# Key maxima and square sums placed among the value tiles, scatters placed beside late gathers, logit groups placed anew

## The reference, cut to what matters

```python
# attention over random features; dn = 64 ** -0.25
dash = einsum('bhnd,md->bhnm', data * dn, proj)
diag = 0.5 * dn ** 2 * sum(data * data, axis=-1)
stab = max(dash, -1) if is_query else max(dash, (-2, -1))   # keys: one maximum per head
feature = ratio * (exp(dash - diag - stab) + EPS)

# graph attention, edges src -> dst
msg = xl[src] + xr[dst]
e = einsum('ehd,hd->eh', where(msg > 0, msg, 0.2 * msg), att)
alpha = softmax of e over the edges of each dst
out = segment_sum(alpha * xl[src], dst) @ W_up
```

## Time and profile before

| what | us |
|---|---|
| median of three runs | 1893.53 |
| lowest and highest | 1887.46, 1898.96 |
| the profiled execution, whole | 1897.03 |
| its span on the core | 1895.2 |
| TensorE busy in it | 1792.2 (95%) |
| VectorE, ScalarE, GpSimd busy | 744.7, 390.4, 644.6 |

### The profile page before, as it was taken

How to read it: one execution, slowest core, us unless ns; L and a number is a source line. 1 busy time by engine, 2 the same in 40 slices (tenths; PEclk the granted TensorE clock), 3 DMA queues, 4 the chain that set the end, 5 groups by cost and what they waited for, 6 DMA issues and landing times. The chain is left out here.

```text
span 1895.2 us, 22157 instructions
## 1 busy us (share of the span) xinstructions
PE 1792.2 (95%) x8594; PEld 1140.2 (60%) x8594; DVE 744.7 (39%) x1523; ACT 390.4 (21%) x715; POOL 644.6 (34%) x538
## 2 busy tenths in 40 slices
PE   7999999998999999999999999999999999999953
PEld 5466445544554777546677765677654676676731
DVE  5967101332524322454455557340530223222226
ACT  0000000001401011001576745211000312222222
POOL 0566881030000076777887620000300222222210
PEclk9999999999999999999899999999999999999986
DMA  9645115073530144333222145150321799999952
GB/s 344 182 113 144 2 2 155 22 223 66 214 129 5 32 123 133 92 96 86 54 54 53 37 101 154 45 223 24 102 94 45 253 415 407 401 411 410 404 161 88
DMA packets 104070, 289.09 MB, mean 153 GB/s; under 512 B 61942, under 2 KB 65240, under 8 KB 91837
## 3 DMA queue, kind: packets, MB, share of 16 engines
q1 hardware_dynamic: 28634, 224.83, 32.1%
q0 software_dynamic: 68160, 51.85, 12.3%
q10 hardware_dynamic: 7198, 11.36, 1.9%
HBM read 257.19 MB, written 30.32 MB: 152 GB/s over the span
## 5 line engine op out<-in xcount | busy, mean ns | idle before, releaser
L325 PE MATMUL bank<-wring,turned_a 128*125 128x512 f32 x480 | 207.6, 593 | 1.6 <-DVE turned_a L640 0.7
L523 POOL DMA_INDIRECT table_d<-wring x85 | 174.5, 2053 | 97.8 <-issue 63.3
L886 POOL DMA_INDIRECT wring<-xl_d,wring x85 | 109.1, 1284 | 256.4 <-DMA xr_d<-flat_b 230.5
L325 PEld LDWEIGHTS bank<-wring,turned_a 128*125 128x125 f32 x480 | 89.6, 188 | 115.3 <-issue 114.2
L2154 PEld LDWEIGHTS bank<-picked_t,wring 128*128 128x128 f32 x1280 | 145.3, 194 | 7.6 <-issue 7.3
L2154 PE MATMUL bank<-picked_t,wring 128*128 128x128 f32 x1280 | 147.2, 278 | 0.1
L341 PE MATMUL bank<-flat_d,wring 128*128 128x312 f32 (+1 forms) x512 | 135.0, 426 | 0.0
L899 POOL DMA_INDIRECT score_d<-wring x85 | 110.8, 1303 | 69.7 <-DMA score_d<-wring 47.0
L886 POOL DMA_INDIRECT wring<-xr_d,wring x85 | 111.9, 1317 | 25.9 <-issue 25.9
L341 PEld LDWEIGHTS bank<-flat_d,wring 128*128 128x128 f32 x512 | 96.7, 189 | 37.9
L2169 PE MATMUL bank<-wring,unit_t 128*128 128x512 f32 x160 | 74.0, 605 | 0.0
(11 more groups left out here) (433 smaller groups left out, 2764.8 us busy)
## 6 DMA issues: line engine op xcount, KB each, us to landing
wring<-in_experts SPq DMA_DIRECT2D x60, 2048.0 KB, 13.1
wring<-in_L_Ws SPq DMA_DIRECT2D x6, 2048.0 KB, 19.3
table_d<-eq_buf SPq DMA_DIRECT2D x2, 3072.0 KB, 30.1
score_d<-no_edge SPq DMA_DIRECT2D x2, 3072.0 KB, 33.3
wring<-table_d POOLq DMA_DIRECT2D x10, 610.4 KB, 7.3
wring<-score_d SPq DMA_DIRECT2D x5, 1093.8 KB
wring<-pid_d ACTq DMA_DIRECT2D x17, 312.5 KB
wring<-in_edge_w ACTq DMA_DIRECT2D x17, 312.5 KB
```

The lines of the kernel that those rows point to most:

```text
L325: ins = pe.matmul(bank[0:R, :], act_t[:, k, tok(t)], w[:, k * HALF:(k + 1) * HALF], start=(k == 0), stop=(k == chunks - 1))
L523: pool.indirect_dma_start(out=tables_d[b % 2], out_offset=bass.IndirectOffsetOnAxis(ap=edge_at[:, b:b + 1], axis=0), in_=edge_sums[:, b, : ...
L886: pool.indirect_dma_start(out=to[:, g % 2, j, :], out_offset=None, in_=table, in_offset=bass.IndirectOffsetOnAxis(ap=index[:, b:b + 1], ax ...
```

## The change

It has four parts.

- **Key maxima.** Ten key products follow each of the first eight value tiles, none the last two. The loop over value tiles is written out on both engines, and TensorE waits for all keys ahead of the first tile.
- **Square sums.** Keys come first. For each pair of chunks the squares are the moving operand, in two pieces of 313 and 312 columns, and 64 columns of `pair_sel` the weights; the two chunks of the pair go to the lower and the upper 64 rows of a bank. One pair follows the key products of each of the first eight tiles (32 products in all). VectorE copies the sums (`keep_sums`) after tiles 3 and 7, TensorE turns them (`turn_sums`) after tiles 5 and 8, and VectorE sorts them into `neg_k` and `neg_q`. The chain of the maximum stands around tiles 8 and 9.
- **Gathers and scatters.** GpSimd gathers blocks 10 to 39 without scatters. From block 40 on there is a scatter ahead of each gather, as long as the scatters stay ten blocks behind; the rest follow at the end.
- **Logit groups.** Groups 0 to 7 stand ahead of the value tiles, group 8 behind tile 4, group 9 behind tile 8, groups 10 to 16 in attention from u = 2, 12, 22, 33, 45, 58 and 70.

```diff
@@ -846,7 +846,7 @@
-SCATTER_LAG = 13
+SCATTER_FROM, SCATTER_LAG = 40, 10
@@ -870,19 +870,23 @@
+sums = context_flat[:, 0:N]
...
-def gather_block(pool, b):
+def gather_block(pool, b, beside=None):
...
+        if beside:
+            beside()
@@ -937,8 +941,8 @@
-SEL = 100
+SEL = 64
@@ -963,18 +967,21 @@
-KMAX_U = HEADS * T // (2 * T)
+KMAX_U, KMAX_TILES = 2 * T, K
...
-QK_GROUPS = 5
-V_GROUP_AT = {1: 5, 3: 6, 6: 7, 8: 8}
+QK_GROUPS = 8
+V_GROUP_AT = {4: 8, 8: 9}
...
-LATE_STEP_AT = {2 + 10 * g + 2 * n for g in range(GROUPS_E - LATE_GROUP) for n in range(4)}
+LATE_STARTS = (2, 12, 22, 33, 45, 58, 70)
+LATE_STEP_AT = {first + 2 * n for first in LATE_STARTS for n in range(4)}
+SUMS_BANK = {0: 4, 1: 6}
@@ -1121,7 +1128,6 @@
-            pe.wait_ge(s_emptied, keys_made)
@@ -1129,27 +1135,60 @@
-        pe_gemm_rows(pe, x1_t, beside=key_products)
-        pe.wait_ge(v1_set, 5)
-        for side in range(2):
+        def square_sums(pair):
+            pe.wait_ge(squared.sem, 2 * pair + 2)
+            side, at_sel = pair // 4, 6 - 2 * (pair % 4)
+            for n, (at, cols) in enumerate(TOKEN_PIECES):
+                for g in range(2):
+                    ins = pe.matmul(banks[SUMS_BANK[side] + n][g * SEL:(g + 1) * SEL, 0:cols],
+                                    pair_sel[:, at_sel:at_sel + SEL], sq[:, g, at:at + cols],
+                                    start=(pair % 4 == 0), stop=(pair % 4 == 3))
+            ins.then_inc(squares_used, 1)
+        def turn_sums(side):
+            pe.wait_ge(sums_kept, 2 * side + 2)
...
-            for k in range(K):
-                pe.wait_ge(squared.sem, side * K + k + 1)
-                at = HEADS - 2 - 2 * k
-                for t in range(T):
-                    ins = pe.matmul(bank[0:R, t * SEL:(t + 1) * SEL], sq[:, k % 2, tok(t)],
-                                    pair_sel[:, at:at + SEL], start=(k == 0 and t == 0), stop=(k == K - 1),
-                                    skip_group_check=True)
-                ins.then_inc(squares_used, 1)
-            pe.wait_ge(squares_used, (side + 1) * K)
-            pe.sem_inc(d_filled, 1)
-        pe.wait_ge(hmax_made, 1)
-        bank = dring.produce(pe)
-        pe.transpose(bank[0:HEADS, 0:R], hmax[:], ident[0:R, 0:R]).then_inc(d_filled, 1)
-        pe.wait_ge(gdiag_made, 1)
-        bank = dring.produce(pe)
-        pe.matmul(bank[0:R, 0:HEADS], ones[0:HEADS, 0:R], gdiag[:], start=True, stop=True)\
-            .then_inc(d_filled, 1)
+            for t in range(T):
+                ins = pe.transpose(bank[0:R, t * 72:(t + 1) * 72], sums[0:72, tok(t)], ident[0:72, 0:72])
+            ins.then_inc(d_filled, 1)
+        def value_tile(bank, w, t, ks):
+            for k in ks:
+                ins = pe.matmul(bank[0:R, :], x1_t[:, k, tok(t)], w[:, k * HALF:(k + 1) * HALF],
+                                start=(k == 0), stop=(k == K - 1))
+            return ins
+        pe.wait_ge(s_emptied, keys_made)
+        for n in range(2 * T):
+            if n % T == 0:
+                w = wt.take(pe)
+            if n < 2 * T - 1:
+                value_tile(dring.produce(pe), w, n % T, range(K)).then_inc(d_filled, 1)
+            else:
+                spread = dring.produce(pe)
+                bank = dring.produce(pe)
+                value_tile(bank, w, n % T, range(4))
+                pe.wait_ge(gdiag_made, 1)
+                pe.matmul(spread[0:R, 0:HEADS], ones[0:HEADS, 0:R], gdiag[:], start=True, stop=True)\
+                    .then_inc(d_filled, 1)
+                value_tile(bank, w, n % T, range(4, K)).then_inc(d_filled, 1)
+            if n % T == T - 1:
+                wt.free(dring.filled, dring.made)
+            if n == 0:
+                pe.wait_ge(v1_set, 5)
+            if n < KMAX_TILES:
+                key_products(n)
+                square_sums(n)
+            if n == T:
+                turn_sums(0)
+            if n == KMAX_TILES:
+                pe.wait_ge(hmax_made, 1)
+                bank = dring.produce(pe)
+                pe.transpose(bank[0:HEADS, 0:R], hmax[:], ident[0:R, 0:R]).then_inc(d_filled, 1)
+                turn_sums(1)
@@ -1262,15 +1301,24 @@
-        for b in range(2 * GB, EB + SCATTER_LAG):
-            if b < EB:
-                gather_block(pool, b)
-            if b >= SCATTER_LAG:
-                scatter_block(pool, b - SCATTER_LAG)
+        for b in range(2 * GB, SCATTER_FROM):
+            gather_block(pool, b)
+        scattered = [0]
+        def scatter_next(limit):
+            if scattered[0] < limit:
+                scatter_block(pool, scattered[0])
+                scattered[0] += 1
+        for b in range(SCATTER_FROM, EB):
+            gather_block(pool, b, beside=lambda: scatter_next(b - SCATTER_LAG))
+        while scattered[0] < EB:
+            scatter_next(EB)
@@ -1422,34 +1470,59 @@
+        def keep_sums(side):
+            v.wait_ge(squares_used, 4 * side + 4)
+            for n, (at, cols) in enumerate(TOKEN_PIECES):
+                v.tensor_copy(sums[:, at:at + cols], banks[SUMS_BANK[side] + n][:, 0:cols]).then_inc(sums_kept, 1)
+        def keep_negs(neg):
+            turned = dring.consume(v)[0:R, 0:T * 72].rearrange("r (t c) -> r t c", c=72)
+            grouped = neg.rearrange("r t (j g i) -> r t g j i", g=2, i=2)
+            for g in range(2):
+                ins = v.tensor_copy(grouped[:, :, g, :, :], turned[:, :, g * SEL:g * SEL + 8]
+                                    .rearrange("r t (j i) -> r t j i", i=2))
+            ins.then_inc(d_emptied, 1)
+            v.wait_ge(d_emptied, dring.taken)
...
-        for n, (t, cols, bank) in enumerate(rows_tiles(v)):
+        for n in range(2 * T):
+            t, cols = n % T, slice(n // T * HALF, (n // T + 1) * HALF)
+            if n == 2 * T - 1:
+                bank = dring.consume(v)[0:R, 0:HEADS]
+                v.tensor_tensor(neg_k[:], neg_k[:], bank.unsqueeze(1).to_broadcast([R, T, HEADS]),
+                                ALU.subtract).then_inc(d_emptied, 1)
+                v.wait_ge(d_emptied, dring.taken)
+                v.sem_inc(negs_made, 1)
...
-                          bank.rearrange("r (h d) -> r h d", d=DH)).then_inc(d_emptied, 1)
-            for u in range(n * KMAX_U, (n + 1) * KMAX_U):
-                product = dring.consume(v)
-                h, t_key = kmax_unit(u)
-                v.tensor_reduce(kmax[:, t_key, h:h + 1], product[0:R, 0:M], AX.X, ALU.max)\
-                    .then_inc(d_emptied, 1)
+                          dring.consume(v)[0:R, :].rearrange("r (h d) -> r h d", d=DH)).then_inc(d_emptied, 1)
+            if n < KMAX_TILES:
+                for u in range(n * KMAX_U, (n + 1) * KMAX_U):
+                    product = dring.consume(v)
+                    h, t_key = kmax_unit(u)
+                    v.tensor_reduce(kmax[:, t_key, h:h + 1], product[0:R, 0:M], AX.X, ALU.max)\
+                        .then_inc(d_emptied, 1)
+            if n == 3:
+                keep_sums(0)
+            if n == T:
+                keep_negs(neg_k)
+            if n == KMAX_TILES - 1:
+                keep_sums(1)
+                v.wait_ge(d_emptied, dring.taken)
+                v.tensor_reduce(hmax[:], kmax[:].rearrange("r t h -> r h t"), AX.X, ALU.max).then_inc(hmax_made, 1)
+            if n == KMAX_TILES:
+                bank = dring.consume(v)
+                dve_step.mark(v.tensor_reduce(gmax[:], bank[0:HEADS, 0:R], AX.X, ALU.max))
+                after(v, dve_step)
+                v.sem_inc(d_emptied, 1)
+                v.tensor_scalar(gdiag[:], ident[0:HEADS, 0:HEADS], gmax[:, 0:1], None, ALU.mult)\
+                    .then_inc(gdiag_made, 1)
+                keep_negs(neg_q)
...
-        for neg in (neg_q, neg_k):
-            bank = dring.consume(v)[0:R, 0:T * SEL].rearrange("r (t h) -> r t h", h=SEL)[:, :, 0:HEADS]
-            v.tensor_copy(neg[:], bank).then_inc(d_emptied, 1)
-        v.wait_ge(d_emptied, dring.taken)
-        v.tensor_reduce(hmax[:], kmax[:].rearrange("r t h -> r h t"), AX.X, ALU.max).then_inc(hmax_made, 1)
-        bank = dring.consume(v)
-        dve_step.mark(v.tensor_reduce(gmax[:], bank[0:HEADS, 0:R], AX.X, ALU.max))
-        after(v, dve_step)
-        v.sem_inc(d_emptied, 1)
-        v.tensor_scalar(gdiag[:], ident[0:HEADS, 0:HEADS], gmax[:, 0:1], None, ALU.mult).then_inc(gdiag_made, 1)
-        bank = dring.consume(v)[0:R, 0:HEADS]
-        v.tensor_tensor(neg_k[:], neg_k[:], bank.unsqueeze(1).to_broadcast([R, T, HEADS]),
-                        ALU.subtract).then_inc(d_emptied, 1)
-        v.wait_ge(d_emptied, dring.taken)
-        v.sem_inc(negs_made, 1)
@@ -1605,10 +1678,10 @@
-        for side, buf in enumerate((q1_t, k1_t)):
+        for side, buf in enumerate((k1_t, q1_t)):
...
-                    s.wait_ge(squares_used, side * K + k - 1)
+                    s.wait_ge(squares_used, (side * K + k) // 2)
```

(30 more changed lines are left out.)

## The result

The changed kernel takes 1914.51 us (median of four runs, 1913.16 to 1916.46); the kernel before took 1895.24 beside it. The ratio is 1.0104, 95% interval 1.0083 to 1.0126: slower by about 19 us, outside the predicted range of 1882 to 1910. In the profiled executions the spans are 1914.6 and 1895.2.

The account below looks back on a forecast made before the run. TensorE was taken to set the pace, but GpSimd's late gathers to place attention: start 4.7 us earlier, attention's end 6 later, 2.3 saved at the scores, total +4, or 1897.5 us against the median; range 1882 to 1910.

Parts of the forecast that it names:

- The first copy: VectorE's copy of the first value tile, behind the logits of groups 0 to 7: VectorE free at 795.7, 10.8 us later.
- sums of 1.27 us per tile: Square sums on TensorE: some 1.2 us per tile if column halves overlap; 2.3 per tile would prove the forecast wrong.
- the waits at loads: GpSimd's scatters held by the loads of Wo's second half and W_up: about 6.5 us each.
- late adds that wait: VectorE in attention waiting for late gathers: 5.2 us for group 12 and 4.3 for group 13.
- the score wait of 5.89: VectorE's wait for scores after attention in the kernel before, 5.89 us: expected to go, with TensorE's 2.33 behind it.
- the 1.5 that I had added for the clock: Attention's start moved from 899.0 to 900.5, because TensorE's idleness ahead of 796 lowers its clock.
- The late gathers: GpSimd's DMAs for groups 10 to 13, the deciding term: group 13 lands at 993.3, so attention ends 6 us later.
- the bound above: Upper limit of a scatter's wait for the previous scatter to land on GpSimd: 0.2 us per pair of scatter and gather.
- rival (3): Each GpSimd pair waits for its scatter to land, 0.2 more over 59 pairs: 12 us later, 1909.5; chance 0.2.
- 2.5 us for a lower clock: TensorE in attention: about 2.5 us added because two waits for late groups lower its clock.
- rival (2): Gathers keep up because loads don't hold scatters: group 13 lands at 980, nothing waits, 8 us less, 1885.5; chance 0.23.
- TensorE sets the pace: Kernel before: TensorE busy 100.19 of 103.55 us in value tiles and 172.10 of 174.60 in attention, so it bounds both.

Follow-up runs that it names:

- the adds fitted: The changed kernel with only the places of the late groups' adds moved, to u = 2, 15, 30, 45, 57, 67, 75: 1897.13 us, ratio 1.0026.
- both fits: The changed kernel with seven groups instead of eight ahead of the value tiles, and late adds placed where gathers should have landed: 1891.26 us, ratio 0.9996.
- W_up last: Seven groups ahead and late adds refitted, against that kernel: W_up and xl loaded behind the first four score loads, last four groups' adds earlier: 1885.23 us, ratio 0.9971.

## Why the prediction was wrong

**Right.** The first copy (800.85, less the 3.34 us of lateness 797.5; predicted 795.7 in the sum), TensorE idle ahead of it (11.66), sums of 1.27 us per tile (1.2 predicted), the waits at loads (4.44 and 1.32, then 2.53 and 5.27, 13.6 us in all; predicted 13), late adds that wait, and the score wait of 5.89 gone. Attention started at 907.13, 903.8 on the scale of before; predicted 900.5. Of the 3.3 us between, 1.8 are the later copy. The other 1.5 lie in the stretch behind it: its tiles took 11.85 us each (807.21 to 819.06) where 11.5 was summed, some 3 us in all, against the 1.5 that I had added for the clock.

**Wrong: the sum of "The late gathers".** The mechanism was there and its size was not. Group 13's add was to wait for a landing at 993.3 and started at 1013.64, 17.0 us later than predicted after the 3.34 are taken off. Group 11's add, summed as in time, waited 3.87 us, and group 12's 10.54 where 5.2 was summed. The working:

- The scatters start 1.8 us late, since eighty gathers took 1.62 us each (662.45 to 792.06) and not 1.597 (127.8 us).
- 4.2 us is the wait at 901.24 for group 9's add. It had no term: I had counted where adds wait for gathers, but not where gathers wait for adds.
- The holds at loads are 0.6 more than predicted.
- What is left, 10.4 us over 59 pairs, is 0.18 per pair. Added up from GpSimd's rows, the waits away from the loads, beyond the 0.3 us that stands ahead of every issue, are 14.2 us, 0.24 per pair. By either count it is about the bound above, 0.2, and not the nothing to 0.05 that I took. I had the row for it, 3.23 us for a scatter behind a gather, and argued it away by the age of the gather. The first ten pairs, without such holds, took 3.38 each, against 3.16.

So rival (3), each pair waits for its scatter, is nearest to what happened, with the time of 1909.5 that it named still 5 too low: the wait for group 9's add is not in it either.

**Wrong: the clock and the logits.** A late add costs more than its wait. I allowed 2.5 us for a lower clock, and TensorE's busy time in attention grew by 6.46; with the adds fitted and no waits it was 200.74, not above the 202.25 of before. And the scatters waited 20.3 us in all for logits, not at most one (4.08 at 1088.69 and 16.20 at 1117.42). In this kernel that cost nothing that shows on TensorE, as attention ended later still.

**The rule that made rival (2).** The holds at loads are shown by rows: 4.44 us at 856.11, and 5.27 at 918.73, which was gone when W_up's load was moved. With both fits such a hold (6.25) went from 899.75 to 1065.15 (5.21) with the load. By the Trainium skill (DMA: Bandwidth & Descriptors, SWDGE vs HWDGE vs iDMA) a DMA engine round-robins between the queues of the two kinds, by which I had allowed that a scatter slips in; by these rows, if it does, it is not without cost. Which part of a scatter the load delays stays open.

**The frame.** "TensorE sets the pace" left out a bound that my own rows held: in the kernel before TensorE already waited 2.33 us for scores. I had counted on attention ending later; had it ended earlier, as in rival (2), the kernel would have met that bound. This is shown by the adds fitted alone (1897.1) and with seven groups (1891.3), where rival (2) promised 1885.5.

## What to carry to other kernels

When work moves between queues, write the landing time of each late transfer beside the time at which its user stands in the order, in both directions: users that wait for data, and transfers that wait for a buffer. Place the users by measured landings; seven numbers were worth some 15 us here. Where one engine wins time, look for the next chain that is nearly as long, and shorten it in the same change: 13 us won on TensorE were worth nothing that could be measured until the scatters ended earlier.

## What was unexpected of the hardware

- Eight fp32 matmul instructions of 312 or 313 columns in alternate column halves took 1.27 us, and 1.28 when both pieces of one half came before the other half's, where eight in full width would take 2.16 by the 6.47 us of 24. The gain does not depend on neighbours alternating; that it is an overlap of the halves is not shown.
- A scatter of 125 rows kept the next one waiting up to 6.25 us while W_up (1024.0 KB) and the copy of `xl` behind it were under way, at each of the two places where they stood among scatters. Behind the 2048 KB of Wo's second half, issued at 831.44 in the kernel with W_up last, it was 7.41 us (842.42). That row names VectorE, but it is scatter 15, whose logits were done before the value tiles.
- A scatter followed by a gather costs 3.38 us, where two gathers cost about 3.2 and a scatter behind a scatter 2.84: where the landing is waited for anyway, the gather beside a scatter adds only 0.5 us. (The 3.38 is a mean with one long issue of 2.02 in it.)
- TensorE's granted clock was 0.77, 0.86 and 0.85 in the three stretches whose adds waited, and 0.99 in the one after, with no wait. The first of these is not the waits' doing: attention's first stretch had 0.74 in the kernel before and 0.78 with the adds fitted, both with no add waiting. Behind it the fitted kernel had 1.00 to attention's end, the changed one 0.94. The same 1520 instructions took 3% longer than before.
